# Routed experts of a mixture: from dense products over all tokens to sorted tiles of chosen rows

## What is computed

```python
x = x + xattn(layernorm(x), ctx, ctx, Wq, bq, ...)        # 16 heads of 16
h = layernorm(x).reshape(1600, 256)
scores = sigmoid(h @ gate_w.T)                             # 32 experts
sc = scores + gate_bias
# 8 groups of 4 experts: the 4 groups whose best two sum highest; then the top 8 experts of those
tki = top_k(masked(sc), 8)[1]
tkw = take_along_axis(scores, tki); tkw = 2.5 * tkw / (tkw.sum() + 1e-20)
combine = scatter of tkw to 32 columns (0 elsewhere)
g = silu(einsum('th,eih->tei', h, w_gate)); u = einsum('th,eih->tei', h, w_up)
routed = einsum('tei,ehi->th', g * u * combine[:, :, None], w_down)     # inner width 128
shared = silu(h @ sh_gate.T) * (h @ sh_up.T) @ sh_down.T                # inner width 256, as two of 128
out = x + routed + shared
```

## Time and profile before

| | |
|---|---|
| Median of 2 runs | 689.49 us (688.76 to 690.22) |
| Profiled execution, its own time | 689.38 us |
| Its span, first to last instruction | 687.6 us |
| Mean granted clock of TensorE | 0.975 |
| Busy: PE / DVE / ACT / POOL | 625.4 / 559.5 / 271.4 / 249.4 us |
| Moved by DMA | 61.66 MB |

### The profile page before, as it was taken

The page is one execution under the profiler, slowest core; times in us unless marked ns, Lnnn a source line. Parts: engine busy times, 40 slices in busy tenths (PEclk is TensorE's granted clock), DMA queues, the critical chain, the costliest instruction groups (busy, mean ns, idle before and its releaser), DMA issues.

```text
span 687.6 us, 13004 instructions
## 1 busy us (share of the span) xinstructions
PE 625.4 (91%) x4232; PEld 569.0 (83%) x4232; DVE 559.5 (81%) x942; ACT 271.4 (39%) x590; POOL 249.4 (36%) x222
## 2 busy tenths in 40 slices
PE   3897999997589999999999999999999999999996
PEld 3885666664489898999999899999999999999995
DVE  5967999994748888888888888888888888888885
ACT  3444665652123333333333333333333333333331
POOL 6530334344013333333333333333333333333332
PEclk9999999998779999999999999999999999999998
DMA  6210000000123343433334343444343433333341
GB/s 192 80 59 1 2 2 3 2 2 0 49 74 94 98 133 97 122 111 113 120 101 131 95 125 109 131 120 125 102 131 94 130 104 119 115 102 132 95 123 49
DMA packets 33373, 61.66 MB, mean 90 GB/s; under 512 B 4008, under 2 KB 14768, under 8 KB 33348
## 3 DMA queue, kind: packets, MB, share of 16 engines
q1 hardware_dynamic: 33348, 61.31, 29.6%
HBM read 59.44 MB, written 1.86 MB: 89 GB/s over the span
## 4 chain that ended last, share of the span: by engine, by line
PE 76%; DVE 16%; issue 5%; ACT 1%; DMA 1%; POOL 0%; SPq 0%; DVEq 0%
PE ps L647 47%; PE ps L813 24%; DVE prob L498 4%; DVE rden L519 3%; DVE nm L489 2%; PE ps L834 2%; DVE st L509 1%; DVE xn L445 1%; DMA cst<-consts 1%; DVE ot L521 1%; DVE x_all L507 1%; PE ps L737 1%; PE ps L700 0%; PE ps L710 0%; PE ps L696 0%
## 5 line engine op out<-in xcount | busy, mean ns | idle before, releaser
L302 POOL TENSOR_TENSOR act<-act,cw 128x400 f32<-128x400 f32 x136 | 178.8, 1315 | 328.5 <-DVE act L595 328.5
L647 PE MATMUL ps<-h_hi_all,w_hi 128*128 128x400 f32 x544 | 189.0, 347 | 4.9 <-DVE w_lo L544 4.9
L393 ACT ACTIVATE act<-ps 128x400 f32<-128x400 f32 x136 | 68.5, 504 | 311.6 <-PE ps L647 311.6
L647 PE MATMUL ps<-h_lo_all,w_hi 128*128 128x400 f32 x544 | 188.9, 347 | 0.0
L647 PE MATMUL ps<-h_hi_all,w_lo 128*128 128x400 f32 x544 | 188.6, 347 | 0.0
L592 DVE SCALAR_TENSOR_TENSOR act<-act,ps 128x400 f32<-128x400 f32 x136 | 77.7, 571 | 83.5 <-ACT act L393 83.5
L813 PE MATMUL ps<-a_hi,w_hi 128*128 128x400 f32 x272 | 99.2, 365 | 19.5 <-issue 17.0
L647 PEld LDWEIGHTS ps<-h_hi_all,w_hi 128*128 128x128 f32 x544 | 103.2, 190 | 5.0 <-issue 5.0
L647 PEld LDWEIGHTS ps<-h_lo_all,w_hi 128*128 128x128 f32 x544 | 103.3, 190 | 0.0
L647 PEld LDWEIGHTS ps<-h_hi_all,w_lo 128*128 128x128 f32 x544 | 103.2, 190 | 0.0
L544 DVE TENSOR_TENSOR w_lo<-w_raw,w_hi 128x512 fp32r<-128x512 f32 x68 | 102.9, 1513 | 0.0
(11 more groups left out here) (118 smaller groups left out, 664.7 us busy)
## 6 DMA issues: line engine op xcount, KB each, us to landing
cw<-combine_rows SPq DMA_DIRECT2D x68, 400.0 KB, 4.0
w_raw<-w_exp SPq DMA_DIRECT2D x68, 256.0 KB, 3.9
w_raw<-w_exp SPq DMA_DIRECT2D x68, 128.0 KB, 2.0
x_all<-x SPq DMA_DIRECT2D x4, 400.0 KB
ctx_f<-ctx_t SPq DMA_DIRECT2D x4, 400.0 KB, 3.7
out_t<-y_out SPq DMA_DIRECT2D x8, 200.0 KB, 2.0
wa<-w_attn SPq DMA_DIRECT2D x4, 256.0 KB, 6.1
cst<-consts SPq DMA_DIRECT2D x1, 266.0 KB, 5.7
```

The source lines that it names most:

```text
L302: pool.tensor_tensor(act[:, s, :], act[:, s, :], cw[:, (s // 2) % 2, (s % 2) * TG:(s % 2 + 1) * TG], ALU.mult).then_inc(weighted, 1)
L393: a.activation(act[:, s, :], ps[:, 4 + 2 * (s % 2), 0:TG], ACT.Tanh, scale=0.5).then_inc(tanh_e, 1)
L647: last = t.matmul(out, w, m, start=(i == 0), stop=(i == n - 1))
```

## The change

The routed experts no longer run on all tokens. While attention goes on, DVE routes two batches at a time (`route`), PE counts by small products how many tokens have gone to each expert so far (`positions`), and DVE turns that into eight places per token in a table `slots` in device memory, in which every expert has its own stretch (`destinations`). POOL writes each batch's normalised rows, with the token's number and its 32 weights behind the 256 numbers (289 in all), to these places with eight indirect DMAs of 100 rows (`rows_to_experts`). After the last batch SP closes each expert's stretch with 128 rows of padding, whose token numbers point to rows that nobody reads.

The weights of all 32 experts (12.6 MB) are loaded once into SBUF during attention (`experts_load`). The two shared experts run on all tokens as plain fp32 products between attention and the loop (`shared_gate_up`, `shared_down`).

Then 132 tiles of 128 rows run. The count is fixed; tiles beyond the last real one read padding. Which expert a tile has and where its rows begin is in a table `tab`, from which SP and PE load registers. Per tile: SP loads the rows (`tin`) and the column of this expert's weights (`wcol`) into one of 12 slots; PE turns the rows (`turn_tile`), DVE copies them out; PE makes gate and up for 128 rows with the rows as weights and 256 columns moving (`gate_up`, plain fp32, no split); ACT and DVE apply silu and the weight; PE turns the result (`turn_act`), ACT copies it out; PE does `down`; ACT copies 128 rows of 256 into one of four `ysb` buffers (`rows_done`), and POOL adds them with an accumulating indirect DMA to the rows of one of four sums in device memory, tile j to sum j % 4. The add of a tile waits for the one of four tiles earlier. Sum 0 starts with the tokens after attention, sums 1 to 3 with zeros. At the end SP loads the four sums back, PE adds and turns them, DVE adds the shared experts' part, and the result is stored.

The normalised rows are no longer split, nor are the experts' weights; q, k and v have a tensor for each group of batches, with the same instructions. Cut to its core (`+` lines of `route` and of the preparation of the tables are left out):

```diff
-    comb = nc.dram_tensor("combine_rows", (NX, T), F32).ap()
+    slots = nc.dram_tensor("slots", (DUMMY + P, ROW), F32).ap()
+    sums = [nc.dram_tensor(f"sums{i}", (SINK + P, D), F32).ap() for i in range(NSUM)]
...
+            def experts_load(first, end):
+                sp.dma_start(w_all[:, first:end, :], w_exp[2 + first:2 + end].rearrange("e p n -> p e n")).then_inc(expert_in, 16)
...
-            def gate_up_load(e, slot):
-                sp.dma_start(w_raw[:, slot, 0:2 * D],
-                             w_exp[bass.ds(e, 1), :, 0:2 * D].rearrange("o p n -> p (o n)")).then_inc(wr_in[slot], 16)
...
-            for slot in range(2):
-                gate_up_load(slot, slot)
-                down_load(slot, slot)
-            attention_over(sp)
-            for slot in range(2):
-                combine_loads(0, slot, slot)
-
-            sp.wait_ge(cmbt_ready, 2)
-            sp.dma_start(comb[NX - NE:NX, :], comb_t[:]).then_inc(cmb_out, 16)
-            sp.wait_ge(cmb_out, 16)
-            def pair_loads(h, e):
-                for slot in range(2):
-                    E = h * NX + e + slot
-
-                    wait_alone(sp, gu_lo, E - 1, half_ready, 1)
-                    gate_up_load(e + slot, slot)
-                    wait_alone(sp, dn_lo, E - 1, half_ready, 1)
-                    down_load(e + slot, slot)
-                    wait_alone(sp, weighted, CPH * (E - 1), half_ready, 1)
-                    combine_loads(h, e + slot, slot)
...
+            sp.dma_start(w_sh[:], w_exp[0:2].rearrange("e p n -> p e n")).then_inc(shared_in, 16)
+            sp.wait_ge(tables_ready, 1)
+            sp.dma_start(slots[DUMMY:DUMMY + P, :], pad[:]).then_inc(pad_out0, 16)
+            sp.dma_start(sums[0][SINK:SINK + P, :], pad[:, 0:D]).then_inc(zero_out, 16)
+            for i in range(1, NSUM):
+                sp.dma_start(sums[i][0:13 * P, :].rearrange("(c p) d -> p c d", p=P),
+                             pad[:, 0:D].unsqueeze(1).to_broadcast([P, 13, D])).then_inc(zero_out, 16)
+                sp.dma_start(sums[i][13 * P:, :], pad[0:P // 2, 0:D]).then_inc(zero_out, 16)
...
+            experts_load(0, 6)
+            for g, (first, end) in enumerate(((6, 11), (11, 17), (17, 23), (23, 30))):
+                sp.wait_ge(pv_psum, BG * (g + 1))
+                experts_load(first, end)
+                sp.wait_ge(x1_ready, BG * (g + 1))
+                sp.dma_start(by_token(sums[0][g * TG:(g + 1) * TG, :]), x_all[:, g * BG:(g + 1) * BG, :]).then_inc(x1_out, 16)
...
+            sp.wait_ge(pad_ready, 1)
+            for b in range(XR):
+                sp.wait_ge(rows_out[b], 16 * TOPK * (NB // XR))
+            for e in range(NE):
+                at = sp.value_load(pad_at[0:1, e:e + 1], min_val=e * CAP, max_val=e * CAP + T)
+                sp.dma_start(slots[bass.ds(at, P), :], pad[:]).then_inc(pads_out, 16)
+            sp.wait_ge(pads_out, 16 * NE)
+            sp.wait_ge(pad_out0, 16)
+            sp.wait_ge(table_ready, 2)
+
+            def tile_loads(q, s):
+                j = q * RING + s
+                at = sp.value_load(tab[0:1, 1, bass.ds(j, 1)], min_val=0, max_val=DUMMY)
+                e = sp.value_load(tab[0:1, 0, bass.ds(j, 1)], min_val=0, max_val=NE - 1)
+                if not isinstance(q, int):
+                    sp.wait_ge(added[s % NSUM], 16 * ((q - 1) * (RING // NSUM) + s // NSUM + 1))
+                sp.dma_start(tin[:, s, :], slots[bass.ds(at, P), 0:ID + 1]).then_inc(row_in[s], 16)
+                sp.dma_start(wcol[:, s:s + 1], slots[bass.ds(at, P), bass.ds(e + WT, 1)],
+                             allow_slow_non_contiguous=True).then_inc(row_in[s], 16)
+
+            for s in range(RING):
+                tile_loads(0, s)
+            with sp.Fori(1, ROUNDS) as q:
+                for s in range(RING):
+                    tile_loads(q, s)
...
+            for a in range(NSUM):
+                sp.wait_ge(added[a], 16 * (TILES // NSUM))
...
+            for g in range(NG):
+                if g >= 2:
+                    sp.wait_ge(fin_psum, KC * (g - 1))
+                for a in range(NSUM):
+                    sp.dma_start(fin[:, g % 2, a], by_token(sums[a][g * TG:(g + 1) * TG, :])).then_inc(fin_in[g % 2], 16)
...
             def second_norm(B):
+                if B >= XR:
+                    pool.wait_ge(rows_out[B % XR], 16 * TOPK * (B // XR))
+                pool.iota(xr[:, B % XR, ID:ID + 1].bitcast(I32), [[1, 1]], base=B * S, channel_multiplier=1).then_inc(id_ready, 1)
...
+            def rows_to_experts(B):
+                pool.wait_ge(dest_ready, B // 2 + 1)
+                for r in range(TOPK):
+                    pool.indirect_dma_start(slots[:], bass.IndirectOffsetOnAxis(ap=dest[:, B % XR, r:r + 1], axis=0),
+                                            xr[:, B % XR, :], None).then_inc(rows_out[B % XR], 16)
...
             for B in range(NB):
                 second_norm(B)
...
+                if B >= 5:
+                    rows_to_experts(B - 5)
+            for B in range(NB - 5, NB):
+                rows_to_experts(B)
...
+            for j in range(TILES):
+                pool.wait_ge(yt_ready, j + 1)
+                if j >= NSUM:
+                    pool.wait_ge(added[j % NSUM], 16 * (j // NSUM))
+                pool.indirect_dma_start(sums[j % NSUM][:], bass.IndirectOffsetOnAxis(ap=tin[:, j % RING, ID:ID + 1].bitcast(U32), axis=0),
+                                        ysb[:, j % YR, :], None, compute_op=ALU.add).then_inc(added[j % NSUM], 16)
...
+            def rows_done(j, q, s):
+                a.wait_ge(yt_psum, j + 1)
+                if not (isinstance(j, int) and j < YR):
+
+                    a.wait_ge(added[s % NSUM], 16 * (q * (RING // NSUM) + s // NSUM))
+                a.activation(ysb[:, s % YR, :], ps[:, 6 + s % 2, 0:D], ACT.Copy).then_inc(yt_ready, 1)
...
+            for i in range(NB):
+                maximum(i)
+                differences(i)
+                if i >= 2:
+                    residual(i - 2)
+                if i >= 6 and i % 2 == 0:
+                    route(i // 2 - 3)
+                if i >= 1:
+                    v.wait_ge(pv_psum, i)
+                    if i >= 7 and i % 2 == 1:
+                        positions_read((i - 7) // 2)
+                    outputs_scaled(i - 1)
+                if i >= 7 and i % 2 == 1:
+                    destinations((i - 7) // 2)
...
+            def rows_turned(j, s):
+                v.wait_ge(lt_psum, j + 1)
+                if not (isinstance(j, int) and j < 2):
+                    v.wait_ge(gu_psum, j - 1)
+                v.tensor_copy(hts[:, s % 2], ps[:, s % 2, 0:KC * P].rearrange("p (k t) -> p k t", k=KC)).then_inc(lt_ready, 1)
+
+            def gate(j, s):
+                v.wait_ge(tanh_e, j + 1)
+                v.scalar_tensor_tensor(opened_t[:, 2 + s % 2, :], opened_t[:, s % 2, :], 1.0, ps[:, 2 + s % 2, 0:FI], ALU.add,
                                        ALU.mult).then_inc(opened, 1)
...
+            def turn_tile(q, s, j):
+                if not (isinstance(j, int) and j < 2):
+                    t.wait_ge(lt_ready, j - 1)
+                t.wait_ge(row_in[s], 32 * (q + 1))
+                for k in range(KC):
+                    last = t.transpose(ps[:, s % 2, k * P:(k + 1) * P], tin[:, s, k * P:(k + 1) * P], ident)
+                last.then_inc(lt_psum, 1)
+
+            expert = lambda j: t.value_load(tab[0:1, 0, bass.ds(j, 1)], min_val=0, max_val=NE - 1)
+
+            def gate_up(j, s, e):
+                t.wait_ge(lt_ready, j + 1)
+                if not (isinstance(j, int) and j < 2):
+                    t.wait_ge(gated, j - 1)
+                w = w_all[:, bass.ds(e, 1), 0:2 * D].rearrange("p o (t k n) -> p k (o t) n", t=2, k=KC)
+                for k in range(KC):
+                    last = t.matmul(ps[:, 2 + s % 2, 0:2 * FI].rearrange("p (t n) -> p t n", t=2), hts[:, s % 2, k, :], w[:, k],
+                                    start=(k == 0), stop=(k == KC - 1))
                 last.then_inc(gu_psum, 1)
 
-            def down(k, s, experts):
-                slot = s // 2
-                if s % 2 == 0:
-                    t.wait_ge(dn_hi, experts)
-                    t.wait_ge(dn_lo, experts)
-                t.wait_ge(a_hi_ready, k + 1)
-                t.wait_ge(a_lo_ready, k + 1)
+            def turn_act(j, s):
+                t.wait_ge(gated, j + 1)
+                if not (isinstance(j, int) and j < 2):
+                    t.wait_ge(at_ready, j - 1)
+                t.transpose(ps[:, 4 + s % 2, 0:P], act_t[:, s % 2, :], ident).then_inc(at_psum, 1)
+
+            def down(j, s, e):
+                t.wait_ge(at_ready, j + 1)
+                if not (isinstance(j, int) and j < 2):
+                    t.wait_ge(yt_ready, j - 1)
+                t.matmul(ps[:, 6 + s % 2, 0:D], ats[:, s % 2, :], w_all[:, bass.ds(e, 1), 2 * D:].rearrange("p o n -> p (o n)"),
```

(33 more changed lines are left out.)

804 lines of the change are left out of this document (450 added, 354 removed).

## The result

The changed kernel takes **769.35 us** (median of 2 runs, 768.52 to 770.18) against 689.49 before: ratio 1.116, 95% interval 1.109 to 1.123. It is slower by 80 us. 658 was predicted, so the direction was wrong; the time lies just inside the range of 575 to 770. The profiled execution took 768.52 us for a span of 766.6.

The account below looks back on a forecast made before the run. PE passes over all 1600 tokens for 34 experts were taken to bound the expert stage, about 505 us. Sum: 112 + 175 + 2 + 34 + 6 + 277 + 5 + 45 + 1.8 = 658 us; range 575 to 770.

Parts of the forecast that it names:

- The scatter: POOL's indirect row writes after the first destinations at 112 us: 175 us of work plus 2.0 landing, last row in memory at 289 us.
- c: POOL's price for issuing one indirect DMA, taken as 1.2 us (0.34 to 2.84), for the row writes and the adds.
- Rival 3: POOL pays more per indirect DMA: slower than before from 1.44 us each; at 1.8 the total is 735 us; chance 0.13.
- Pads: After the scattered rows land, SP does 32 register loads and dynamic DMAs, 0.70 + 0.35 us each: 34 us.
- T = 2.1: Period of each of 132 loop tiles in us, set by SP's two register loads and two dynamic issues: 277 us.
- Rival 2: SP becomes the loop's engine: register load 0.70 us, tile 2.8 us, pads 45 us, total 762 us; chance 0.16.
- The end: After the loop: last tile 5 us, then loading four sums, adding on PE and storing 45 us, or 60 at half clock.
- Rival 4: Chain of adds: one needing over 8.1 us to land stalls ACT in `rows_done`; at 10 us total 750; chance 0.07.
- rival 5: The clock: gaps in the loop keep PE at 1.2 GHz, 3.44 us per tile, total 835 us; chance 0.05.
- rival 6: Whether work is not reduced: 16,896 rows replace 34 x 1600 = 54,400, PE's loop falls to 227 us; no chance given.
- Rival 1: POOL and SP cheaper than their nearest rows: 0.85 us per indirect DMA, loop near 1.8 us per tile, total 566; chance 0.22.
- three signs of being wrong: Loop waits in `rows_done`, PE's share there under 0.6, or POOL's price per indirect DMA outside 0.9 to 1.5 us.

## Why the prediction was wrong, step by step

In the profiled execution 768.5 - 658 = 110.5 us are to be found. They are four differences: 21 in the scatter, 5 in the pads, 64 in the loop, 21 at the end. That the time still lies inside the stated range is due to the range, which reached far into "slower"; it is no merit of the sum.

- **First destinations, 112 us**: POOL's first write began at 109.3. Right.
- **The scatter, 289 us**: SP's wait for it ended at 309.5. The price c was the open term: taken 1.2, measured 0.99 and 0.30 between two, 1.29; 12 us more over 128. The rest of the queue (307.7 - 109.3 - 128 x 1.295) is 33 us where 21 were taken for `second_norm`: POOL waits 13.6 us for DVE's destinations, and DVE's in turn came 20 us earlier with half the writes. The landing took 1.9, as taken. The mechanism was right (half the writes end it at 251); the size was low by 21. Rival 3 asked for c = 1.44 and was not met: the 128 writes took 0.98 to 1.24 us, nothing near 3.1. The case of the Trainium skill's sentence ("SBUF — State Buffer", Who interferes with whom), a DVE copy that holds the shared port, is not tested by that: the one COPY that DVE made from 109 to 308 us reads PSUM.
- **Pads, 34 us**: 39.4, from 309.5 to 348.9. SP's first issue came only at 313.1, after single pieces of 0.69 us (start, length):

```profile
309.51 0.03 SPq L284
...
309.58 0.48 SPq L286
...
310.32 0.69 SPq L286
...
312.42 0.69 issue
...
313.12 0.00 SPq L287
```

  From there a pad takes 1.15 us where 1.05 was taken, for two wrong parts: an issue costs 0.58, not 0.70, and a load 0.55, not 0.35.
- **T = 2.1, "SP sets the pace by a little"**: this is the step that failed. SP does set the pace, but not by a little, and its stream was costed too low: "I take one register load at r = 0.35". Measured r = 0.55 to 0.58, half of it the two bound checks, which the listing of SP's instructions shows behind each load and the sum counted at nothing. The issue was taken too dear, 0.70 for 0.58, which hid half of it; 2 x 0.58 + 2 x 0.55 = 2.26, and 2.25 was measured in the first tiles. The loop proper adds 0.27 (2.52). There the tile's number is a register and not a constant, and the trace shows two pieces of register arithmetic with each load in place of one (252 FUSED_REGOPS for 132 loads, twelve of them before the loop); the turn of the loop adds some 0.6 us every twelve tiles. At 132 tiles 0.42 us too little is 55 us. The other 9 are the way of the first tile to its add, 11.1 us (354.4 to 365.5) less one period, for which no term stood.
- **Rival 2** is what happened. Its own sum of 762 had r = 0.70 and T = 2.8, over both; its break-even of 0.455 was passed. The Trainium skill's floor for a register load ("DMA: Bandwidth & Descriptors", Latency and other measured facts), 600 ns, is close to the 0.55 and 0.58 of a load with its checks. As a floor for the load itself it is not what this case shows: the TENSOR_LOAD rows have 0.27, and so has a load without checks. By the Trainium skill's figure the sum was 732. It was the better of the two estimates for T (2.6 against 2.52), and got a chance of 0.16 because the only row near it was taken as the value and not as a bound.
- **PE 1.72, POOL 1.2, DMA 1.3 a tile**: none of them mattered at T = 2.52, but all were low (DMA by its share with all checks gone: 0.84 x 1.95 = 1.64). An add on POOL costs 1.55 + 0.30 = 1.85, half a microsecond over a plain indirect write, and PE is busy 190.83/200 x 1.95 = 1.86 us for a tile. Had SP been free, T would have been 2.02 (static addresses), and the time some 66 us less than measured, 703 by estimate, the same as before within what can be told, and not the forecast's gain.
- **The end, 45 us**: 71.3 from the last add, where 50 stood (5 and 45). The sum had "or 60 with PE at half clock", and the clock is what happened: 0.50 from 710 on, a pass every 0.214 us where 0.117 was taken from the earlier trace rows at the clock regained there. That is 14 us of the 21: 54.9 of passes where 33 and 7.5 stood. Most of the rest is the first load's landing, 9.6 us (699.1 to 708.7) where 2 was taken. PE had been busy 3.1 of 20 us before, and then 57 us in which it was 94% busy did not bring the clock back. Moving the adds off PE gave 20 us and not the 40 by which PE's work fell; then the 6.4 MB of loads are what is late.
- **Rival 4** fell (POOL waits for no add), **rival 5** fell in the loop (granted clock 1.00 at PE 80% busy) and came true at the end, **rival 6** held: PE's work is less. **Rival 1** was wrong in both parts.
- None of the three signs of being wrong showed. The loop doesn't wait in `rows_done`, PE's share there is 0.80, and c is 1.29 from one to the next. They watched PE, the adds and c, and none watched r, on which T hung.
- Chances: "slower" had 0.30. The forecast leaned on three prices with no row (c, r, the add), each taken at or below its nearest row, and all three came out higher.

## What to carry to other kernels

A loop with addresses from registers can be bound by the engine that issues. Count its instructions one by one, bound checks too, and hold their sum against the busy engines' before anything else. The profile doesn't count them as busy and the waits don't name them; the view of their own line does show them. To find such a bound, add one instruction of the suspected kind to each of two engines: the one where the time rises by its full price is the pacer. Here half of SP's cost for register loads were run-time checks of numbers that the program had clamped itself. Without them alone the change is level with before (696 us); with one load for each tile, three sums and the adds on DVE as well it pays (650 us, or 0.942 of before). The price is that a wrong number would no longer be caught.

## What the runs showed of the hardware

- With the pads ahead of the wait, while POOL issued indirect writes back to back, SP's moves and issues took up to 0.70 us each, and its dynamic issues came 6.9 us apart and not 1.1. In the kernel after SP's first pad still took 3.5 us, after the scatter had landed. There ACT ran nothing for 43.6 us and DVE for 29.5, though PE's last products before that were through at 284.8; both went on within half a microsecond of the end of POOL's last write (307.65). In order of time (start, length, idle before and what ended it):

```profile
306.66 0.99 POOL L367 DMA_INDIRECT slots<-xr,dest  x1 [0.30 <-issue]
307.56 0.50 ACT L464 ACTIVATE sh_act<-ps 128x400 f32<-128x400 f32 x1 [43.61 <-remote]
308.10 0.57 DVE L688 SCALAR_TENSOR_TENSOR sh_act<-sh_act,ps 128x400 f32<-128x400 f32 x1 [29.50 <-issue]
```

  With half the writes ACT's wait was 18.1 us. So it is shorter with a shorter scatter, but its end is not tied to the last write: ACT went on at 245.8 there, with four writes still to come. By what way the two hang together stays open, and no run tells the loading of instructions from anything else. It costs little while the pads follow the scatter and hide it, and is why bringing them forward gave nothing.
- An indirect write of 100 rows of 1156 bytes holds POOL for 0.99 us, an adding one of 128 rows of 1 KB for 1.55, and 0.30 pass between two. They were not compared at one size.
- The granted clock was 0.75 from 109 to 245 us with PE busy 102 of 136, where attention before had 1.00.
